# The memory stage of a four-layer attention kernel: pooling done a phase earlier, products in two banks, and P^T copied first in the self-attention's tail

## What is computed

```python
pooled = rms_norm(mem_out.mean(axis=1), mem_pool_norm_w)      # mem_out is ctx_1024
mem_tok = broadcast_to((pooled @ to_mem_tokens_w)[:, None, :], (b, NM, DIM))
_, k_c, v_c = jnp.split(mem_tok @ to_qkv_w, 3, axis=-1)
...
kf = concatenate([k_extra, pm, k], axis=2)                    # 16 memory tokens, 16 persistent, own
vf = concatenate([v_extra, pm, v], axis=2)
probs = softmax(where(mask, q @ kf.T * DH ** -0.5, -1e30))
attn_out = (probs @ vf).reshape(b, n, HEADS * DH) @ to_out_w
```

## Time and profile before

| | us |
|---|---|
| median of 3 runs | 2415.65 (2414.92 to 2417.21) |
| the profiled execution | 2419.09 |
| its span, first to last instruction | 2417.3 |
| PE busy in the span | 2249.4 (93%) |
| PE weight loads | 1876.4 (78%) |
| DVE busy | 1862.4 (77%) |
| POOL busy | 1567.2 (65%) |
| ACT busy | 1495.6 (62%) |

### The profile page before, as it was taken

How to read it: one execution, slowest core, us unless ns; L and a number is a source line. 1 busy time by engine, 2 the same in 40 slices (tenths; PEclk the granted TensorE clock), 3 DMA queues, 4 the chain that set the end, 5 groups by cost and what they waited for, 6 DMA issues and landing times.

```text
span 2417.3 us, 90082 instructions
## 1 busy us (share of the span) xinstructions
PE 2249.4 (93%) x30214; PEld 1876.4 (78%) x30214; DVE 1862.4 (77%) x4063; ACT 1495.6 (62%) x3472; POOL 1567.2 (65%) x2374
## 2 busy tenths in 40 slices
PE   7999999978888888999999989999999999999799
PEld 5777778966666666777778968888888888888688
DVE  4888881159999996777775678899999999998465
ACT  5888885558888886888885524444444444444343
POOL 2666663139999994666667766666666666666333
PEclk9999999979999998999999989999999999999999
DMA  4111112245555542222221223333333333333121
GB/s 131 45 44 44 45 49 66 68 121 166 169 167 168 164 138 49 52 51 51 51 55 55 68 74 92 95 96 96 96 96 96 97 96 97 95 96 95 53 63 54
DMA packets 443731, 211.95 MB, mean 88 GB/s; under 512 B 206704, under 2 KB 434545, under 8 KB 443505
## 3 DMA queue, kind: packets, MB, share of 16 engines
q1 hardware_dynamic: 443632, 210.69, 32.5%
HBM read 113.54 MB, written 29.88 MB: 59 GB/s over the span
## 4 chain that ended last, share of the span: by engine, by line
PE 55%; POOL 16%; issue 12%; SPq 8%; DVE 4%; ACT 3%; DMA 1%; POOLq 0%; DVEq 0%; ACTq 0%
PE bank L1179 6%; PE bank L1453 6%; PE bank L701 5%; PE bank L1540 5%; PE bank L661 5%; PE bank L1193 4%; POOL sb_region L1038 4%; PE bank L721 3%; POOL sb_rstd L1055 3%; PE bank L1493 3%; SPq L1399 3%; SPq L1402 3%; POOL sb_z L1059 3%; PE bank L1479 2%; PE bank L1517 2%
## 5 line engine op out<-in xcount | busy, mean ns | idle before, releaser
L1739 POOL TENSOR_TENSOR sb_pn<-sb_l,sb_r_all 128x512 f32<-128x512 f32 x128 | 134.8, 1053 | 269.7 <-DVE sb_r_all L1670 228.0
L892 DVE TENSOR_REDUCE sb_max<-bank 128x8 f32<-128x616 f32 x256 | 203.3, 794 | 136.6 <-PE bank L675 69.5
L701 PE MATMUL bank<-sb_ident,sb_region 128*77 128x128 f32 x2048 | 274.5, 277 | 33.5 <-ACT sb_pT L798 32.2
L785 ACT ACTIVATE sb_region<-sb_region 128x616 f32<-128x616 f32 x384 | 276.0, 719 | 22.3 <-POOL sb_region L1038 20.8
L798 ACT ACTIVATE sb_pT<-bank 77x1024 f32<-77x1024 f32 x256 | 261.0, 1020 | 41.9 <-PE bank L701 41.8
L701 PEld LDWEIGHTS bank<-sb_ident,sb_region 128*77 128x77 f32 x2048 | 236.7, 152 | 62.1 <-issue 42.5
L897 DVE TENSOR_TENSOR sb_region<-bank,sb_max 128x616 f32<-128x616 f32 x256 | 204.6, 799 | 18.3
L721 PE MATMUL bank<-sb_pT,sb_v 77*32 77x128 f32 x6144 | 208.8, 276 | 2.8 <-ACT sb_pT L798 2.1
L721 PEld LDWEIGHTS bank<-sb_pT,sb_v 77*32 77x32 f32 x6144 | 155.6, 109 | 71.2 <-issue 65.1
L661 PE MATMUL bank<-sb_region,sb_qT 32*128 32x308 f32 x1536 | 158.8, 483 | 54.5 <-ACT sb_region L813 21.8
L1595 ACT ACTIVATE sb_oT<-bank 128x512 f32<-128x512 f32 x128 | 76.5, 598 | 213.9 <-PE bank L1507 213.9
(11 more groups left out here) (186 smaller groups left out, 6455.9 us busy)
## 6 DMA issues: line engine op xcount, KB each, us to landing
sb_region<-in_side SPq DMA_DIRECT2D x64, 616.0 KB, 3.8
sb_pT<-sb_region SPq DMA_DIRECT2D x512, 64.0 KB, 2.0
sb_kF<-sb_region SPq DMA_DIRECT2D x512, 64.0 KB, 2.1
scratch_after_A<-sb_y SPq DMA_DIRECT2D x256, 64.0 KB, 1.7
sb_fx<-scratch_after_A SPq DMA_DIRECT2D x96, 128.0 KB, 2.1
sb_mask<-in_mask SPq DMA_DIRECT2D x64, 154.0 KB, 2.3
sb_x<-scratch_after_F SPq DMA_DIRECT2D x128, 64.0 KB, 1.9
sb_ctx<-in_ctxT SPq DMA_DIRECT2D x192, 38.5 KB, 1.9
```

The costliest lines, as they stand in the source:

```text
L701: mm = nc.tensor.transpose(two[0:C, h * T:(h + 1) * T], p_s[b.par][:, head * C:(head + 1) * C], ident[:])
L785: nc.scalar.activation(half(p_s[b.par], k), half(p_s[b.par], k), ACT.Exp, scale=SCALE[ph]).then_inc(exp_made.sem(b), 1)
L892: nc.vector.tensor_reduce(dst, by_bank_and_head(scores_half(k)), AX.X, ALU.max).then_inc(max_made.sem(b), 1)
```

## The change

Three parts. **Pooling**: PE's transpose of sumT and DVE's mean and square move into A0's tail (t = 0 of `between`), POOL's two steps ahead of F0, DVE's two scalings (`pool_norms`) into what DVE does ahead of F0; PE waits ahead of F0 until the mean is read. **Memory stage**: PE no longer waits for F0's last sum there (a wait in A1's own first steps stays); it starts with the pooled transpose; persistent values and angles go to banks 4 and 5; values are made ahead of keys and counted by themselves, so that PE waits for the values' copy alone before the products; the products of the two heads of a pair go to one bank, at partitions 0 to 63 and 64 to 127, in banks 4 and 5; ACT copies them in two pieces of 128 partitions and PE does not wait for that. The transfers to HBM go by half of the heads, in pieces of 512 bytes. **Self-attention's tail**: in steps 62 and 63 ACT copies P^T before the exponentials.

```diff
             transpose_p(b, 1)
-    drive(pe, NB, step, reach=REACH)
+    def between(t):
+        if ph == "A0" and t == 0:
+            turn_sums(pe)
+    drive(pe, NB, step, reach=REACH, between=between)
...
             statistics(b + -2)
-    drive(dve, NB, step_weighted if ph == "A1" else step, reach=REACH)
+    def between(t):
+        if ph == "A0" and t == 0:
+            pool_mean(dve)
+    drive(dve, NB, step_weighted if ph == "A1" else step, reach=REACH, between=between)
...
                 keep_outputs(b + -1, h)
-            if has(0):
+            if has(0) and has(2):
                 exps(b, h)
...
                 keep_p(*half_before(b, h))
+            if has(0) and not has(2):
+                exps(b, h)
             if has(1):
...
 memT = sb("memT", [D, NB])
-vomem_sb = [fh_s[s][0:NB, :, :].rearrange("b f t -> b (f t)") for s in range(2)]
+vomem_sb = fh_s[0][:].rearrange("p f t -> p (f t)")[:, 0:H // 2 * D]
 angles = [l_s[1][:, n * T:(n + 1) * T] for n in range(2)]
...
-def pool_vector(dve):
+def pool_mean(dve):
     dve.wait_ge(sums_turned, 1)
...
+def pool_norms(dve):
     dve.wait_ge(pool_step, 4)
...
 def memory_tensor(pe):
-    last = Batch(GROUPS // 2 - 1, 1)
-    pe.wait_ge(ft_made.sem(last), ft_made.count("F0", last))
+    pe.wait_ge(pool_step, 6)
+    nc.tensor.transpose(bank[0][:, 0:NB], scaled[:], ident[0:NB, 0:NB]).then_inc(mem_poolT, 1)
     for c in range(H // 2):
         row, col = 32 * (c % HC), c // HC * D
-        mm = nc.tensor.matmul(bank[7][row:row + 32, col:col + D], persT[:, c, :], wout3[:, c, :], start=True, stop=True)
+        mm = nc.tensor.matmul(bank[4][row:row + 32, col:col + D], persT[:, c, :], wout3[:, c, :], start=True, stop=True)
     mm.then_inc(vopers_made, 1)
+    pe.wait_ge(mem_poolT_kept, 1)
+    nc.tensor.matmul(bank[1][:, 0:NB], wmem[:], poolT[:], start=True, stop=True).then_inc(mem_tok, 1)
     pe.wait_ge(angles_spread, 2)
     for n in range(2):
-        mm = nc.tensor.transpose(bank[6][:, n * T:(n + 1) * T], angles[n], ident[:])
+        mm = nc.tensor.transpose(bank[5][:, n * T:(n + 1) * T], angles[n], ident[:])
     mm.then_inc(angles_turned, 1)
-    pe.wait_ge(pool_step, 6)
-    nc.tensor.transpose(bank[0][:, 0:NB], scaled[:], ident[0:NB, 0:NB]).then_inc(mem_poolT, 1)
-    pe.wait_ge(mem_poolT_kept, 1)
-    nc.tensor.matmul(bank[1][:, 0:NB], wmem[:], poolT[:], start=True, stop=True).then_inc(mem_tok, 1)
     pe.wait_ge(mem_tok_kept, 1)
+    for c in range(H // 2):
+        col = 2 * HD3 + c * 128
+        mm = nc.tensor.matmul(bank[3][:, c * NB:(c + 1) * NB], wqkv[:, col:col + 128], memT[:], start=True, stop=True)
+    mm.then_inc(mem_kv, 1)
     by_eo = wqkv[:, HD3:2 * HD3].rearrange("p (n f two) -> p n two f", two=2, f=F)
...
                 row = r * KH + eo * F
-                nc.tensor.matmul(bank[2][row:row + F, key_place(c) * NB:(key_place(c) + 1) * NB], by_eo[:, 2 * c + r, eo], memT[:], start=True, stop=True)
-    for c in range(H // 2):
-        col = 2 * HD3 + c * 128
-        mm = nc.tensor.matmul(bank[3][:, c * NB:(c + 1) * NB], wqkv[:, col:col + 128], memT[:], start=True, stop=True)
+                mm = nc.tensor.matmul(bank[2][row:row + F, key_place(c) * NB:(key_place(c) + 1) * NB], by_eo[:, 2 * c + r, eo], memT[:], start=True, stop=True)
     mm.then_inc(mem_kv, 1)
-    pe.wait_ge(mem_kv_kept, 2)
+    pe.wait_ge(vopers_kept, 1)
+    pe.wait_ge(angles_kept, 2)
+    pe.wait_ge(mem_kv_kept, 1)
     for c in range(H // 2):
...
             rows = slice(r * KH, (r + 1) * KH)
-            mm = nc.tensor.matmul(bank[2 * r + c // HC][0:NB, c % HC * D:(c % HC + 1) * D], vmemT[rows, c * NB:(c + 1) * NB], wout3[rows, c, :],
+            mm = nc.tensor.matmul(bank[4 + c // HC][r * NB:(r + 1) * NB, c % HC * D:(c % HC + 1) * D], vmemT[rows, c * NB:(c + 1) * NB], wout3[rows, c, :],
                                   start=True, stop=True)
     mm.then_inc(vomem_made, 1)
-    pe.wait_ge(vopers_kept, 1)
-    pe.wait_ge(vomem_kept, 4)
-    pe.wait_ge(angles_kept, 2)
+    pe.wait_ge(mem_kv_kept, 2)
 def memory_scalar(act):
+    act.wait_ge(mem_poolT, 1)
+    nc.scalar.activation(poolT[:], bank[0][:, 0:NB], ACT.Copy).then_inc(mem_poolT_kept, 1)
     act.wait_ge(vopers_made, 1)
-    nc.scalar.activation(vopers[:], bank[7][:, 0:2 * D], ACT.Copy).then_inc(vopers_kept, 1)
+    nc.scalar.activation(vopers[:], bank[4][:, 0:2 * D], ACT.Copy).then_inc(vopers_kept, 1)
+    act.wait_ge(mem_tok, 1)
+    nc.scalar.activation(memT[:], bank[1][:, 0:NB], ACT.Copy).then_inc(mem_tok_kept, 1)
     act.wait_ge(angles_turned, 1)
     for n, table in enumerate((cosT, sinT)):
-        nc.scalar.activation(table[:], bank[6][:, n * T:(n + 1) * T], ACT.Copy).then_inc(angles_kept, 1)
-    act.wait_ge(mem_poolT, 1)
-    nc.scalar.activation(poolT[:], bank[0][:, 0:NB], ACT.Copy).then_inc(mem_poolT_kept, 1)
-    act.wait_ge(mem_tok, 1)
-    nc.scalar.activation(memT[:], bank[1][:, 0:NB], ACT.Copy).then_inc(mem_tok_kept, 1)
+        nc.scalar.activation(table[:], bank[5][:, n * T:(n + 1) * T], ACT.Copy).then_inc(angles_kept, 1)
     act.wait_ge(mem_kv, 1)
+    nc.scalar.activation(vmemT, bank[3][:, 0:H // 2 * NB], ACT.Copy).then_inc(mem_kv_kept, 1)
+    act.wait_ge(mem_kv, 2)
     nc.scalar.activation(kmemT[:].rearrange("p c b -> p (c b)"), bank[2][:, 0:H // 2 * NB], ACT.Copy).then_inc(mem_kv_kept, 1)
-    nc.scalar.activation(vmemT, bank[3][:, 0:H // 2 * NB], ACT.Copy).then_inc(mem_kv_kept, 1)
     act.wait_ge(vomem_made, 1)
-    for n in range(4):
-        by_pair = vomem_sb[n % 2].rearrange("b (c r d) -> b r c d", r=2, d=D)
-        nc.scalar.activation(by_pair[:, n // 2], bank[n][0:NB, :].rearrange("b (c d) -> b c d", d=D), ACT.Copy).then_inc(vomem_kept, 1)
+    for n in range(2):
+        nc.scalar.activation(vomem_sb[:, n * HC * D:(n + 1) * HC * D], bank[4 + n][:], ACT.Copy).then_inc(vomem_kept, 1)
...
 def memory_sync(sp):
-    sp.wait_ge(vomem_kept, 4)
-    for s in range(2):
-        sp.dma_start(vomem_dram[:, s * HC * 2 * D:(s + 1) * HC * 2 * D], vomem_sb[s]).then_inc(mem_stored, 16)
+    sp.wait_ge(vomem_kept, 2)
+    by_head = vomem_dram.rearrange("b (c r d) -> r b c d", r=2, d=D)
+    for r in range(2):
+        sp.dma_start(by_head[r], vomem_sb[r * NB:(r + 1) * NB, :].rearrange("b (c d) -> b c d", d=D)).then_inc(mem_stored, 16)
...
-    dve.wait_ge(mem_kv, 1)
+    dve.wait_ge(mem_kv, 2)
     for n, what in enumerate("kq"):
...
+    def pooled(pe):
+        rest_loaded(pe)
+        pe.wait_ge(pool_step, 1)
     def before_self(pe):
...
-    def memory(pe):
-        turn_sums(pe)
-        memory_tensor(pe)
-    phases(pe, cross_tensor, ff_tensor, self_tensor, {"F0": rest_loaded, "A1": memory, "A3": before_self})
+    phases(pe, cross_tensor, ff_tensor, self_tensor, {"F0": pooled, "A1": memory_tensor, "A3": before_self})
...
         spread_angles(dve)
+        pool_norms(dve)
         nc.vector.tensor_scalar(key_bias_rows[:], rowmask[:], cross["A1"]["bk"][:, 0:1], None, ALU.mult).then_inc(masks_made, 1)
...
-    phases(dve, cross_vector, feed_forward, self_attention, {"F0": before_ff, "A1": pool_vector, "F2": scale_weights})
+    phases(dve, cross_vector, feed_forward, self_attention, {"F0": before_ff, "F2": scale_weights})
...
     pool.wait_ge(masks_made, 3)
+    def pool_ready(pool):
+        rest_loaded(pool)
+        pool_gpsimd(pool)
     def rms_ahead(t):
...
-    phases(pool, cross_gpsimd, feed_forward, self_gpsimd, {"F0": rest_loaded, "A1": pool_gpsimd})
+    phases(pool, cross_gpsimd, feed_forward, self_gpsimd, {"F0": pool_ready})
...
```

## The result

The changed kernel takes **2401.09 us**, median of 5 runs (2399.78 to 2404.23), against 2414.92 of 5 runs of the kernel before beside it (2411.62 to 2417.21): ratio 0.9947, 95% interval 0.9933 to 0.9962. Its profiled execution took 2403.81 us, with a span of 2402.0 at a mean granted clock of 0.986 (before: 2417.3 at 0.981). Both profiled executions took longer than these medians, the one of before by 4.2 us and the one of after by 2.7.

What follows compares the result with a forecast made beforehand. TensorE or VectorE bounds most of the kernel, except a dependent TensorE-ScalarE chain in the memory stage and the self-attention's tail. Gains of 10.1 + 2.6 = 12.7 us gave a median of 2403.0 us, range 2400.0 to 2407.5.

Steps and rivals of the forecast that it cites:

- (a): Memory stage start: the wait for F0's last sum and the pooling chain go; pooled transpose starts 3.37 us earlier.
- (b): Memory stage: from the pooled transpose to the first product with memT takes 1.33 us, as before.
- R1: Memory stage: clock falls inside the products; 2406.7 us if all run at 1.2 GHz, 2405 if midway; chance 0.13.
- (c): Memory stage: the 16 value products, now first, take 1.8 us at 2.4 GHz; 3.62 at the low clock.
- (d): Memory stage: the 64 key products take 1.5 us at either clock, hiding ScalarE's 0.6 us copy of the values.
- (e): Memory stage: 32 output products take 1.85 us at 2.4 GHz, two halves side by side in one bank; bounds 1.85 and 3.68.
- R2: Memory stage: output-product halves take turns in their shared bank, plus 1.7 us, 2404.7 us; chance 0.05.
- (f): Into the second cross attention: TensorE skips the copies' wait, L631 10.3 us earlier, ScalarE 9.7; gain taken as 10.1 us.
- (g): Second cross attention's ramp: clock falls, returns about 15.7 us after L631; no gain or loss, bounds +1 and -1.1 us.
- R3: Second cross attention's ramp: keeps or regains 2.4 GHz earlier, 1.1 us less, 2401.9 us; chance 0.09.
- R5: Second cross attention: clock stays at 1.2 GHz, losing 4 us a batch, slower overall; chance 0.02, milder form 0.02.
- R4: ScalarE's order still holds TensorE (2405.1 us), or self-attention's tail gives 1.2 us or less (2404.4); chance 0.10.

Runs made afterwards that it cites:

- the gaps filled: Kernel before plus 15 unused filler products in three of TensorE's memory-stage gaps: 2409.33 us, ratio 0.9980.
- pooling late: Changed kernel with the pooling back between F0 and the memory products, other parts kept: 2409.77 us, ratio 0.9979.
- the fillers: Changed kernel with context loads ahead of query loads and unused products in TensorE's gaps in A1's first steps: 2400.65 us, ratio 0.9939.
- the kernel that was held: Changed kernel with TensorE again waiting for both copies of the output products before A1's first batch: 2402.30 us, ratio 0.9948.
- all three additions: Changed kernel plus context loads ahead, fillers in A1's ramp, half of q(63) issued by ScalarE: 2394.92 us; with the old tail order 2397.63 us.
- only the gather changed: Changed kernel with half of the last query gather, q(63), issued by ScalarE instead of SyncE: 2397.80 us, ratio 0.9933.

## Why the prediction held, and where its steps were off

The time forecast was 2403.0 us, in a range of 2400.0 to 2407.5, against 2401.09; the narrow band of 2401.5 to 2404.5 was missed by 0.4 us. The memory stage was right in its mechanism and gave a little more than forecast, the self-attention's tail gave less. That the tail looks right in the one pair of profiles (3.05 us for 2.6) is luck: the profile of before has the longest tail of the four with the old order. By its steps:

- **(a), (b)** right. L1847 starts 3.66 us behind the start of L1199, in the slot that the transpose of sumT had (3.57), and the first product with memT 1.53 us after it, where 1.33 and 0.03 were forecast.
- **The clock, and rival R1.** 1.00 from 490 to 501 us, as forecast; R1 falls. (Between 490 and 495 us the timeline of before has four waits of TensorE, not the five of the prediction; nothing hangs on it.) That gaps ahead of the products make it fall, and nothing in the products themselves, is shown from both sides: with the gaps filled in the old order it stayed, with one gap of 3.10 us in the new order it fell.
- **(c)** 2.00 for 1.8 us: the width of the moving side is 64 here and 128 in L1193, yet a matmul costs 0.125 us (2.00/16) and not less. The pace of L1193 was the right one within a tenth.
- **(d)** was mis-sized: 1.10 us, not 1.5 "in any case". I read 1.51 as one pace at both clocks; it was a mean. At 1.2 GHz throughout, the same 64 take 1.94 us (pooling late), at 2.4 GHz 1.10.
- **(e), and rival R2.** 1.96 for 1.85 us, with the halves in one bank; the same 1.96 in four banks. R2 falls. The sentence of the Trainium skill ("TensorEngine Tiling (Array Packing)", "Gotcha 1: PSUM Pressure") does not hold for two row tiles that write disjoint partitions of one bank, by these two times; R2 had put its price at 1.7 us more.
- **(f)** right. L631 came 10.04 us behind L1199's start, 10.13 forecast; ScalarE's L823 moved by 9.8 (9.7 forecast). The 0.6 us that L661 was to give back if it found 2.4 GHz is there (0.80 for 1.41 us), so VectorE started 10.56 us earlier where I took 10.1. That is the one term that I chose low.
- **(g), and R3, R5.** The clock fell in the ramp and was back 15.7 us behind L631 (15.7 forecast), the fourth weighting kept 10.52 us of the 10.56. R3 and R5 did not come; the fillers show that R3's price, 1.1 us, was of the right size (1.0).
- **R4**: its first half, that ScalarE's order holds TensorE as the wait did, falls by the kernel that was held (L631 1.30 us later). Its second half, a tail that gives 1.2 us or less, nearly came, as the next points show.
- **The first cross attention's tail**: 0 us, right, but VectorE's first sum of F0, which was to be 0.4 us late, was 1.3 late (it began 10.70 us behind the last transposes of A0's results, 9.41 before), by a row that I had not expected (the scaling of 1.42 us, below). The working had a slip as well: GpSimd's first residual at 375.3 and 0.8 us more make 376.1, not 376.7. TensorE had other products to do: from those transposes to F0's last 32 products it took 119.3 us, 119.2 before.
- **Self-attention's tail**: the step that failed in size. 2.6 us was forecast. In the kernels with all three additions, with the clock full up to the second projection, the order gives 2.08, and over all profiles here the stretch is 38.1 us in the four kernels with the old order and the old gathers, and 36.9 in the seven with the new one, 1.3 less. Two causes. First, in the first half it gives 1.48 (1.18 forecast), but in the second only 0.6 more, not 1.4: "their result is wanted only behind the next scores and products" was wrong by 0.81 us, since the exponentials that now come last feed GpSimd's normalisation, which the next transposes wait for. Second, batch 62 gained nothing, as forecast, but a longer wait wasn't free: the bound named it ("more of this stretch falls to 1.2 GHz, which the longer idle time before it may do") and I did not price it. In all seven the wait was 3.37 us or more, and the first products behind it ran at 1.2 GHz (2.6 to 2.7 us from the gated product to the first reduction, against 1.56 at 2.4 GHz); with the old order that happened in two of four.
- **Between the stages**, the shift came through whole, within the scatter of 2 us.

## What to carry to other kernels

A chain of short products between gaps is priced at the clock that its gaps leave it: price each operation at both clocks, from rows that lie wholly at one, and count a removed gap with the products behind it. Parts of such a change need not add up, since one remaining gap can lose what the others saved (0.7 us alone, 6.2 us with the rest in the profiles; 4.6 and 7.7 in the time, with wide intervals). One profile is one execution: where the clock can fall or hold, look whether its time is near the median, or whether the runs fall into two clusters. And where TensorE waits for a transfer, look whether the data or the issuing is late: a queue whose issues stand end to end is an engine like any other, and another engine's idle time can take half of them. A wait that shrinks proves little by itself, for the one who waits may just have come later.

## What the runs showed of the hardware

- **The moment of the clock's fall scatters.** The changed kernel, and the one with only the gather changed, are the same up to there; the granted clock fell 15.5 us behind the start of F0's last products in the one and 13.7 in the other. In both it was back after 10.2 us, in the kernel that was held after 13.7; in the kernel with the pooling late, where it had fallen ahead of 8 us of products, after 6.8.
- **A VectorE operation beside GpSimd.** One scaling of 64x128 took 0.28 us in the memory stage before, with GpSimd idle. Moved to F0's start it took 1.42 us, and 1.44 in the kernel that moved only the pooling, while GpSimd ran two additions:

```profile
375.39 1.40 POOL L1333 TENSOR_TENSOR sb_fxb<-sb_fx,sb_L_xattn_ffb 128x256 f32<-128x256 f32 x2
375.45 1.42 DVE L1835 TENSOR_SCALAR sb_pooled<-sb_pooled,sb_pool_var 64x128 f32<-64x128 f32 x1 [5.34 <-POOL sb_pool_var L1843]
376.91 0.28 DVE L1837 TENSOR_TENSOR sb_pooled<-sb_pooled,_L_xattn_mem_pool_norm_w 64x128 f32<-64x128 f32 x1
...
377.25 0.41 DVE L1278 TENSOR_TENSOR sb_ft<-bank,sb_fxb 128x256 f32<-128x256 f32 x1
```

  It starts 0.06 us behind GpSimd's and ends 0.08 us behind its second addition. The Trainium skill, "SBUF — State Buffer", section "SBUF: two separate sides", says that VectorE, in an operation with a two-port mode or with two SBUF inputs, and GpSimd share a pair of ports as an exclusive lock, and that the later one is blocked for the whole instruction. These rows agree in the delay; that the scaling is such an operation, and why it waited for both additions and not for the first alone, no run here shows.
- **With a full weight, fewer moving columns are not cheaper.** A 128x128 weight against 64 moving columns cost 0.125 us (2.00/16) at 2.4 GHz, where 128 columns in L1199 cost 0.117 (3.73/32).
